# Regrouping the last 104 edge blocks of a graph attention kernel as 48, 32 and 24, with one group's spreads made on GpSimd

## The reference

```python
h = (layernorm(x) @ W).reshape(N, H, C)            # 8 heads of 256
e = leaky_relu(a_src[src] + a_dst[dst], 0.2)
e = exp(e - segment_max(e, dst)[dst])
alpha = e / (segment_sum(e, dst)[dst] + 1e-16)
x = x + segment_sum(h[src] * alpha, dst).mean(heads) + bias
x = x + moe(layernorm(x))                          # 8 experts, top 2, gelu
```

## Time and profile before

| what | value |
|---|---|
| median of 3 runs | 1065.32 us (1064.61 to 1065.62) |
| the profiled execution | 1062.06 us |
| its span in the profile | 1060.3 us |
| PE busy | 706.9 us (67%) |
| DVE busy | 692.1 us (65%) |
| POOL busy | 672.2 us (63%) |
| ACT busy | 355.6 us (34%) |
| mean granted TensorE clock | 0.812 of full |

### The profile page before, as it was taken

The page is one execution under the profiler, slowest core; times in us unless marked ns, Lnnn a source line. Parts: engine busy times, 40 slices in busy tenths (PEclk is TensorE's granted clock), DMA queues, the critical chain, the costliest instruction groups (busy, mean ns, idle before and its releaser), DMA issues.

```text
span 1060.3 us, 16555 instructions
## 1 busy us (share of the span) xinstructions
PE 706.9 (67%) x3746; PEld 630.5 (59%) x3747; DVE 692.1 (65%) x1935; ACT 355.6 (34%) x831; POOL 672.2 (63%) x705
## 2 busy tenths in 40 slices
PE   4981020436556656765676676699999997779984
PEld 2980010425546545664665576688888886668873
DVE  6898138545675665766777787647769878734552
ACT  3720021427544554332231110123232223345552
POOL 5787777777767777777777730344145256656665
PEclk9555555769886887786898888899999999889998
DMA  9634053668766776665565435198986652556663
GB/s 350 202 73 103 11 128 107 198 183 275 246 216 195 226 235 209 183 199 151 182 185 152 136 92 205 42 390 310 345 303 240 257 180 86 127 90 108 104 105 44
DMA packets 97127, 190.11 MB, mean 179 GB/s; under 512 B 24755, under 2 KB 54910, under 8 KB 95912
## 3 DMA queue, kind: packets, MB, share of 16 engines
q0 software_dynamic: 31680, 70.52, 27.2%
q1 hardware_dynamic: 50364, 72.93, 20.3%
q10 hardware_dynamic: 14960, 45.16, 11.1%
HBM read 124.74 MB, written 64.74 MB: 179 GB/s over the span
## 4 chain that ended last, share of the span: by engine, by line
PE 28%; POOL 26%; issue 17%; DVE 12%; DMA 12%; POOLq 2%; ACT 2%; ACTq 1%; DVEq 0%; SPq 0%
POOL ring L697 22%; PE banks L931 12%; PE banks L1052 9%; DMA out<-ring 6%; POOL starts_table L751 2%; DMA ring<-agg_table 2%; PE banks L885 2%; DMA ring<-node_table,idx 2%; DVE ring L1740 1%; POOL out L809 1%; DVE arena L1695 1%; PE banks L872 1%; PE banks L1127 1%; DMA arena<-in_src 1%; POOLq L802 1%
## 5 line engine op out<-in xcount | busy, mean ns | idle before, releaser
L697 POOL DMA_INDIRECT ring<-node_table,idx x392 | 408.9, 1043 | 123.2 <-issue 115.3
L931 PE MATMUL banks<-arena,ring 128*128 128x160 f32 x1568 | 289.7, 351 | 125.8 <-issue 64.0
L931 PEld LDWEIGHTS banks<-arena,ring 128*128 128x128 f32 x1568 | 270.8, 230 | 145.3 <-issue 145.1
L1213 ACT COPY arena<-banks 128x400 f32<-128x400 f32 x200 | 88.5, 494 | 345.5 <-PE banks L931 212.3
L809 POOL DMA_INDIRECT out<-ring x56 | 89.7, 1602 | 51.1 <-DMA out<-ring 27.8
L1052 PE MATMUL banks<-ring 128*128 128x256 f32 x544 | 120.5, 381 | 0.0
L1052 PEld LDWEIGHTS banks<-ring 128*128 128x128 f32 x544 | 102.5, 190 | 13.4
L1695 DVE TENSOR_TENSOR arena<-hot,arena 128x640 f32<-128x640 f32 x98 | 75.2, 822 | 44.0 <-PE banks L931 43.5
L1111 PEld LDWEIGHTS banks<-ring 128*128 128x128 f32 x448 | 63.0, 205 | 13.0 <-DVE ring L1923 9.6
L1111 PE MATMUL banks<-ring 128*128 128x128 f32 x448 | 64.3, 290 | 7.7 <-DVE ring L1923 7.5
L1127 PE MATMUL banks<-arena,ring 128*128 x224 | 64.8, 415 | 4.6 <-issue 4.6
(11 more groups left out here) (388 smaller groups left out, 1094.0 us busy)
## 6 DMA issues: line engine op xcount, KB each, us to landing
agg_table<-arena ACTq DMA_DIRECT2D x100, 400.0 KB, 3.3
ring<-agg_table SPq DMA_DIRECT2D x25, 1600.0 KB, 8.5
ring<-slot_table SPq DMA_DIRECT2D x56, 130.0 KB, 2.6
ring<-node_table,idx POOLq DMA_INDIRECT x392, 3.3
ring<-in_x SPq DMA_DIRECT2D x8, 640.0 KB, 14.2
arena<-in_L_ffn_w SPq DMA_DIRECT2D x16, 256.0 KB, 8.9
node_table<-ring SPq DMA_DIRECT2D x5, 640.0 KB, 5.5
ring<-in_L_gnn_W ACTq DMA_DIRECT2D x1, 2048.0 KB, 8.9
```

Of the source, the lines that this page charges most:

```text
L697: pool.indirect_dma_start(rows[:, b % ROOM, :], None, node_table, bass.IndirectOffsetOnAxis(idx[:, b:b + 1], 0)).then_inc(got[got_of(g)], 16)
L931: m = pe.matmul(columns[:, k, bass.ds(at * (UNIT * H), SPREAD * H)], lhs[:, k * P:(k + 1) * P], weights, start=False, stop=True, skip_grou ...
L1213: act.copy(stage[j][:, k * SLOTS * H:(k + 1) * SLOTS * H], views[k]).then_inc(drained, 1)
```

## The change

`GROUP_PLAN` becomes seven groups of 48, one of 32 and one of 24: nine groups in place of ten. The blocks 288 to 335 are now group 6, 336 to 367 are group 7, and 368 to 391 are group 8, the last. All groups of 48 take the PE steps (5, 9, 12, 12), the group of 32 takes (2, 6, 8, 8). The spreads of group 7 (8 quads) are made by POOL, after its last gather, in a function of its own; `hot` has room for two groups, and DVE goes from `take_alpha(7)` straight to `flags(8)`. In the last group `rescale` and `take_alpha` now come before the spreads, as in the others. Ring slots are shifted by `SLOT0` = 16, so that the last group begins at slot 0; three groups of 48 then wrap around the ring, and DVE adds their scores in two instructions. Some tensors of the projection stage change places, and `over_part(1)` waits for the last block.

```diff
-GROUP_PLAN = ((3, 16),) * 6 + ((2, 16),) * 3 + ((1, 8),)
+GROUP_PLAN = ((3, 16),) * 7 + ((2, 16), (2, 12))
...
+    SLOT0 = -first_of[GROUPS - 1] % ROOM
+    LOOPED = (WHOLE - 1) // 2 * 2 - 2
...
-        at_raw2, at_agg0, at_W = 0, RAW, RAW + AGG
+        at_raw2, at_agg1, at_w1 = 0, RAW, RAW + AGG
+        at_W = LAST_BLOCKS * ROW
...
+            def spreads(g):
+
+                pool.wait_ge(alpha_ready, g + 1)
+                for q in range(blocks_of(g) // QUAD):
+                    quad = first_of[g] // QUAD + q
+                    pool.wait_ge(block_done, (quad - SPREAD_RING + 1) * QUAD + 1)
+                    s = quad % SPREAD_RING * QUAD
+                    pool.tensor_tensor(
+                        spread[:, s:s + QUAD, :].rearrange("p s (d h) -> p s d h", h=H),
+                        hot[:, q * QUAD:(q + 1) * QUAD, :].unsqueeze(3).to_broadcast([BLK, QUAD, SPREAD, H]),
+                        alpha[:, quad * QUAD:(quad + 1) * QUAD, :].unsqueeze(2).to_broadcast([BLK, QUAD, SPREAD, H]),
+                        ALU.mult).then_inc(spread_ready, 1)
...
-            for g in range(2, GROUPS - 2):
+            for g in range(2, GROUPS - 1):
                 far_blocks(g - 2)
                 gather(g, 0, blocks_of(g))
 
-            gather(GROUPS - 2, 0, blocks_of(GROUPS - 2))
-            far_blocks(GROUPS - 4)
-            gather(GROUPS - 1, 0, blocks_of(GROUPS - 1))
-            for g in range(GROUPS - 3, GROUPS):
-                far_blocks(g)
+            now = first_of[GROUPS - 3] - (first_of[GROUPS - 1] - ROOM)
+            gather(GROUPS - 1, 0, now)
+            far_blocks(GROUPS - 3)
+            gather(GROUPS - 1, now, blocks_of(GROUPS - 1))
+            spreads(GROUPS - 2)
+            far_blocks(GROUPS - 2)
+            far_blocks(GROUPS - 1)
...
+                group(g, first_of[g] // ITER, slot_of(first_of[g]), first_of[g] // ITER % 2, blocks_of(g), g + 1,
+                      (5, 9, 12, 12) if g < WHOLE else (2, 6, 8, 8))
...
-                if g < GROUPS - 1:
-                    rescale(g, at, cols)
-                    take_alpha(g)
+                rescale(g, at, cols)
+                take_alpha(g)
+                if g != GROUPS - 2:
                     spreads(g)
-                else:
-                    take_alpha(g)
-                    spreads(g)
-                    rescale(g, at, cols)
...
+                if t == 1:
+                    dve.wait_ge(block_done, NB + 1)
```

More of the change, by code:

```diff
@@ L91, in gat_moe_kernel @@
     assert LOOK_UPS[-1][1] == TILES and H * CHUNKS == P and D == 2 * P and C == D and N < TILES * P
-    assert first_of[GROUPS] == NB and WHOLE % 2 == 0 and LAST_BLOCKS % (2 * QUAD) == 0
+    assert first_of[GROUPS] == NB and LOOPED % 2 == 0 and LAST_BLOCKS % (2 * QUAD) == 0 and SLOT0 % ITER == 0
     assert all(kb == GROUP_KB and ch == CHUNKS for kb, ch in GROUP_PLAN[:WHOLE])
     assert all(kb * ch == SHORT for kb, ch in GROUP_PLAN[WHOLE:-1]) and SHORT % ITER == 0 and SHORT == SPREAD_RING * QUAD
-    assert all(first_of[g] % ROOM + first_of[g + 1] - first_of[g] <= ROOM for g in range(GROUPS))
+    assert all((first_of[g] + SLOT0) % ROOM + first_of[g + 1] - first_of[g] <= ROOM for g in range(GROUPS - 2, GROUPS))
     assert SLOTS * H <= 512 and GB % ITER == 0 and TILES % UNROLL == 0 and NS % ACC_RING == 1
@@ L177, in gat_moe_kernel @@
         o += 2 * D
-        w1_now = [ring[:, o + j * 2 * D:o + (j + 1) * 2 * D].rearrange("p (k n) -> p k n", k=2) for j in range(2)]
-        o += 4 * D
         assert o <= at_x
+        w1_now = [ring[:, at_w1 + j * 2 * D:at_w1 + (j + 1) * 2 * D].rearrange("p (k n) -> p k n", k=2) for j in range(2)]
         o = at_raw2
@@ L457, in rows_of, with slot_of @@
             return TILES - 1 - t
+        def slot_of(b):
+            return (b + SLOT0) % ROOM
         def kb_of(g):
@@ L711, in far_blocks @@
                                 pool.tensor_copy(far_rows[:, j, :].unsqueeze(1),
-                                                 rows[:, bass.ds(i * ITER % ROOM + 2 * s + j, 1), 0:D])\
+                                                 rows[:, bass.ds(slot_of(i * ITER) + 2 * s + j, 1), 0:D])\
                                     .then_inc(far_rows_ready, 1)
@@ L1012, in group @@
                     for q0, q1 in zip(cuts, cuts[1:]):
-                        blocks(it + i, slot + i * ITER, (parity + i) % 2, range(q0 - i * per_iter, q1 - i * per_iter))
+                        blocks(it + i, (slot + i * ITER) % ROOM, (parity + i) % 2, range(q0 - i * per_iter, q1 - i * per_iter))
                         if q1 == turn:
@@ L1027, in _ @@
             per_group = GB // ITER
-            with pe.Fori(0, WHOLE // 2 - 1) as pair:
+            with pe.Fori(0, LOOPED // 2) as pair:
                 for j in range(2):
[L1030 to L1034, removed]
+                    group(2 * pair + j, pair * (2 * per_group) + j * per_group, slot_of(j * GB), (j * per_group) % 2, GB, 0, (5, 9, 12, 12))
+            for g in range(LOOPED, GROUPS - 1):
+                group(g, first_of[g] // ITER, slot_of(first_of[g]), first_of[g] // ITER % 2, blocks_of(g), g + 1,
+                      (5, 9, 12, 12) if g < WHOLE else (2, 6, 8, 8))
             pe.drain().then_inc(whole_done, 1)
             pe.wait_ge(rescaled, GROUPS)
-            blocks(first_of[GROUPS - 1] // ITER, first_of[GROUPS - 1] % ROOM, first_of[GROUPS - 1] // ITER % 2, range(LAST_BLOCKS // QUAD))
+            for b in range(first_of[GROUPS - 1], NB, ITER):
+                blocks(b // ITER, slot_of(b), b // ITER % 2, range(min(ITER, NB - b) // QUAD))
             pe.wait_ge(in_proj_w, 16)
```

30 lines of the change are left out of this document (19 added, 11 removed).

## The result

The changed kernel is slower: a median of 1070.38 us (16 runs) beside 1063.67 us for the kernel before (16 runs), a ratio of 1.0059 with a 95% interval of [1.0042, 1.0075]. The profiled execution took 1068.61 us, its span is 1066.9 us, 6.6 more than before. The forecast was 1075.4 us, with a range of 1066.5 to 1082.

What follows compares the result with a forecast made beforehand. Gathers bound the kernel up to group 5, DVE's rounds from 568.5 on. Later group 6, later steps, interference and six last quads end the blocks 10.1 us later: 1065.32 + 10.1 = 1075.4 us, range 1066.5 to 1082.

Steps and rivals of the forecast that it cites:

- the class: Whole kernel slower by more than 0.2% (2.1 us): own forecast and interference case together, chance 0.84.
- Group 6: Scores of the new 48-block group wait for block 335's gather until 551.2; spreads at 584.8, 16.3 us late.
- PE's steps: Beside group 6, steps (5, 9, 12, 12) return factors one quad later: 2.4 us, bounds 0 and 3.0.
- POOL's spreads: Group 7's spreads on POOL, 1.5 us each: PE reaches group 8's transposes 9.5 us after the weights; no saving on chain.
- the interference: POOL's spreads slow DVE's flags and scores of group 8 on SBUF: seven instructions, 7.8 us, 3.4 on the chain.
- My upper bound, 7.6 on the chain: Every POOL spread stops DVE for its whole length before group 8's scores: 8 x 1.5 - 4.4 = 7.6 us.
- the rival of 1081 to 1085: Interference or a slow POOL spread sets group 7: about +16 to +20 us, chance 0.16.
- The last round: Group 8, transposes to first matmul: 16.0, 8.3, 2.4 and 4.7 us, sum 31.4; PE starts the last group at 679.0.
- The rest at nothing: Extra score additions, over_part(1)'s wait, moved tensors and POOL's bias additions counted as costing no time.
- The median: Runs' median taken as 3.3 us above the profiled execution, so 1072.2 became 1075.4 us.
- Faster: Rival: DVE's rounds hide wholly behind PE's quads after group 6; -7.7 us, 1057.6, chance 0.07.
- No change: Rival: PE sets the pace after group 6; terms at low bounds give +2.3 us, about 1067.6, chance 0.09.

Runs made afterwards that it cites:

- a_old_steps: Changed kernel with PE's steps placed as in the kernel before; 1206.55 us beside 1232.68 for the kernel before, ratio 0.9782.
- a_dve_spreads: Changed kernel with group 7's spreads given back to DVE; 1212.49 us beside 1232.68 for the kernel before, ratio 0.9833; repeated, 0.9842.
- after_again: The changed kernel once more, no edit; 1074.17 us beside 1064.10 for the kernel before, ratio 1.0091.
- after: First profile of the changed kernel against the kernel before; median 1070.38 us beside 1063.67, ratio 1.0059.
- a_skip16_3: Changed kernel without the gathers of blocks 320 to 335, third time; 1202.54 us beside 1222.43 for the kernel before, ratio 0.9855.

## Why the prediction was right, point by point

The sign, the class (slower, 0.84) and the range held, and each step of the mechanism is in the rows; the rise was 6.7 us at the medians where 10.1 was forecast. Times in us; the third column is the profile after.

| step of the prediction | forecast | measured |
|---|---|---|
| gather of block 335 issued | 548.3 | 549.9 |
| scores of group 6 | 551.2 | 552.7 |
| from there to its spreads | 33.6 | 33.6 |
| spreads of 6 to weights of 7 | 49.9 | 49.1 |
| one spread on POOL | 1.5 | 1.53 |
| weights of 7 to the transposes of 8 | 12.9 | 11.2 |
| transposes to pieces | 16.0 | 15.0 |
| pieces to the scaled weights | 10.7 | 10.7 |
| from there to the first matmul | 4.7 | 4.6 |
| six quads | 18.4 | 18.6 |
| the blocks end, against before | +10.1 | +8.2 |

*Group 6.* The wait, its releaser and its length came as said; 1.5 us of its start are POOL's drift (block 287 was already 1.0 later). The steps behind it were copied from group 5 and fit to 0.03 us.

*PE's steps.* I took 2.4 us for the factors that come a quad later. `a_old_steps` measures 2.35, and shows why it isn't the whole quad of 2.96, as I had argued: the rescaling waits for the last quad anyway. But 2.4 was chosen between the bounds 0 and 3.0 and not worked out, so that it fits so closely is luck. Against the kernel before, from scores to rescaling, the round is 1.8 longer (27.44 us, 539.11 to 566.55, and 29.26), and from spreads to weights the whole came 0.8 under the forecast.

*POOL's spreads and the interference.* That the offload saves nothing on the chain was right, though POOL's first three products do stand on it (to 640.26, in front of PE's first two quads), and `a_dve_spreads` gives its price: 0.4 to 0.8 us lost. The interference was mis-sized: I took 7.8 us of DVE's time and 3.4 on the chain. DVE lost 6.4, and PE waited 2.35 for the scores (its row of 646.70). The count of seven instructions held by chance: the first of the flags (L1593) ran ahead of POOL and kept its 0.43, and L1595, which I hadn't counted, was hit. Each lost 0.9 us on average, where I had 1.1. My upper bound, 7.6 on the chain, was far off; the rival of 1081 to 1085 needed it. The way of PE to the transposes was mis-sized too: the terms (1.5, 0.3, 0.9 and two quads at 3.26) make 9.2 us and not the 9.5 that I wrote, and it took 8.8, since PE started 2.0 us after the weights (637.56 against 635.53) and not 2.7. The Trainium skill (SBUF — State Buffer, who interferes with whom) has the shared ports as an exclusive lock, where the one that comes first blocks the other. If every product had blocked DVE for its whole length, the seven beside DVE's 11.1 us would have cost it 10.7 us, and it lost 6.4: that bound isn't borne out. The trace agrees on who is hit: the scans and the two-input operations, not the copies of one element, which stay at 0.15. L1595 has one input tensor and went from 0.30 to 1.34; it is a `tensor_scalar`, which the same section counts among the operations that can take the shared ports.

*The last round.* The transposes to the pieces was the term with bounds 14 and 16; it took 15.0, I had taken the upper one. So the four terms that were off are -1.7 (transposes of 8), -1.0 (pieces), -0.8 (round of 7) and +1.5 (drift), -2.0 in all; the others hold to 0.2, and the end came 1.9 earlier than forecast. Without the drift, which I hadn't forecast, it would have been 3.4 earlier: that the end came so near is in part luck.

*The rest at nothing.* The projection moved as a block: its first transposes (L1063 before, L1089 after) come at 728.59 and 736.78, 8.2 later as well, so the new wait of `over_part(1)` and the moved tensors cost nothing. Later some is given back: the experts' last eight matmuls (L1127, L1153) start at 1044.37 and 1051.58, +7.2, and POOL's last issue at 1052.81 and 1059.44, +6.6. `after_again` doesn't give it back (its span is 11.2 above that of before, its projection 9.1 later), so the 1.6 us may be the spread of single executions; it was not traced.

*The median.* I forecast 5.0 us too much: 1.9 from the blocks, 1.6 from that tail, and 1.5 since the median stood 1.8 us above the profiled execution (1070.38 - 1068.61) and not 3.3.

*What failed among the rivals.* "Faster" needed PE's idle time after 586.4 to stay under 24 us. It began at 587.76, and to 695.3 it is 107.6 us, of which 26 quads of 2.96 take 77.0: 30.6 idle. "No change" needed its three terms at their low bounds, 2.4, 3.4 and 2.0 us less; the steps gave 0.6 less, the interference 1.05 and the pieces 1.0.

## What to carry to other kernels

Before a round is dropped by making groups larger, look up which gather or load the first larger group will wait for: here dropping one round of 31 us was paid with 11.5 us of waiting, 2.4 us of later steps and four more quads behind the last weights. The last weights' time and the work still open behind them have to be added; the earlier start of the last group by 3.1 us was worth less than its 11.3 us more of matmuls. Work handed to an idle engine is worth only what the first engine gets done with the time, and if both work on SBUF, look first at what it takes from the other's instructions.

## What the runs showed of the hardware that was not expected

- POOL's product of 640 float32 elements with two broadcast inputs takes 1.37 to 1.78 us (mean 1.53), DVE's 0.75 in a train of eight; beside it a DVE scan of 0.69 us took 1.48 and 1.67, a scores addition of 192 elements 1.41 instead of 0.36. DVE's figures are the same to 0.02 us in all eight profiles that have the pair.
- The same program can run some 15% longer: the kernel before took 1064 us two times and 1222 to 1234 the four other times that it was timed. It doesn't go by the chip: on chip 0 it took 1232.68 us and later 1064.10. ACT's timeline shows it best, in eight copies that stand one behind the other in the program (L1215 in `after`, L1214 in `a_dve_spreads`); first `after`:

```profile
150.79 0.84 ACT L1215 COPY arena<-banks 128x392 f32<-128x392 f32 x1 [92.14 <-PE banks L948]
151.91 0.91 ACT L1215 COPY arena<-banks 128x392 f32<-128x392 f32 x1 [0.27 <-PE banks L948]
```

then `a_dve_spreads`:

```profile
177.05 0.81 ACT L1214 COPY arena<-banks 128x392 f32<-128x392 f32 x1 [9.68 <-issue]
188.25 0.81 ACT L1214 COPY arena<-banks 128x392 f32<-128x392 f32 x1 [10.39 <-remote]
```

  One copy comes every 1.1 us in the first, and the last five every 11.2 in the second, though PE had done its part of all eight by 165.3 there (the last four transposes at 164.41, for 0.92 us). No instruction in the trace accounts for the gap, and what causes the condition stays open. It doesn't take several changed kernels timed together: `a_skip16_3` was timed with the kernel before alone and was disturbed, `after_again` likewise and was not.
